# Value products of a head pair: one group in beat 4 instead of three groups in beats 0, 2 and 4

## What is computed

```python
def ffn(x):                       # W_fc 512x128, W_proj 128x512
    y = square(relu(x @ W_fc.T)) @ W_proj.T
    mem, spikes = 0, 0
    for _ in range(5):            # spiking neurons
        mem = 0.9 * mem + y - (mem > 1)
        spikes += (mem > 1)
    return spikes / 5
def attn(x):                      # 16 heads of 64, slopes 2**(-(h+1)/2)
    q, k, v = split(x @ w_qkv); q *= 64 ** -0.5
    sim = q @ k.T - abs(i - j) * slope[h]      # causal
    return (softmax(sim) @ v) @ w_out + b_out
x = x + 0.5 * ffn(layernorm(x))
x = x + attn(layernorm(x))
x = x + 0.5 * ffn(layernorm(x))
```

## Time and profile before

| | us |
|---|---|
| median of 3 runs | 1767.83 (1766.23 to 1768.95) |
| span of the profiled execution | 1764.1 |
| PE busy | 1676.8 (95%) |
| DVE busy | 1206.1 (68%) |
| ACT busy | 1289.0 (73%) |
| POOL busy | 920.2 (52%) |

### The profile page before, as it was taken

One profiled execution on the slowest core, in us unless ns is written; L12 is line 12 of the kernel. 1 busy time (PEld: TensorE's weight loads), 2 busy tenths in 40 slices (PEclk: granted clock), 3 DMA queues, 4 the chain that ended last, 5 costly groups with the idle time before them and its releaser, 6 DMA issues.

```text
span 1764.1 us, 39796 instructions
## 1 busy us (share of the span) xinstructions
PE 1676.8 (95%) x10902; PEld 1259.1 (71%) x10902; DVE 1206.1 (68%) x4272; ACT 1289.0 (73%) x3446; POOL 920.2 (52%) x1258
## 2 busy tenths in 40 slices
PE   4899999999999999999999999999999999999996
PEld 3767777677776777767777676776777677677775
DVE  6575776748777585775858768586785848767563
ACT  2687876777877787876877768687777868868781
POOL 2455554555545455545555545465454545546451
PEclk8999999999999999999999999999999999999998
DMA  2555453435434435443545434444443544434430
GB/s 73 114 109 111 85 119 75 102 82 109 101 81 107 89 84 108 92 104 76 105 93 107 96 82 107 90 87 107 90 103 78 109 95 94 102 82 101 94 82 13
DMA packets 80562, 164.80 MB, mean 93 GB/s; under 512 B 12880, under 2 KB 30928, under 8 KB 80208
## 3 DMA queue, kind: packets, MB, share of 16 engines
q1 hardware_dynamic: 80336, 162.12, 42.9%
HBM read 6.88 MB, written 4.19 MB: 6 GB/s over the span
## 4 chain that ended last, share of the span: by engine, by line
PE 69%; DVE 19%; issue 8%; POOL 2%; ACT 1%; DVEq 1%; DMA 1%; SPq 0%; POOLq 0%; ACTq 0%
PE bank L388 12%; PE bank L373 12%; PE bank L343 7%; PE bank L359 7%; PE bank L431 7%; PE bank L360 6%; PE bank L439 6%; PE bank L345 5%; PE bank L344 5%; DVE spikes L615 3%; DVE negsc L558 3%; DVE negmem L621 2%; DVE drive L618 2%; DVE xn L591 1%; DVE rsum L567 1%
## 5 line engine op out<-in xcount | busy, mean ns | idle before, releaser
L911 POOL TENSOR_TENSOR prob<-prob,rsum 128x512 f32<-128x512 f32 (+3 forms) x1024 | 731.7, 730 | 699.9 <-DVE rsum L567 699.6
L799 ACT ACTIVATE prob<-negsc,negmax 128x512 f32<-128x512 f32 (+3 forms) x1024 | 574.4, 565 | 124.2 <-DVE negmax L558 117.7
L810 ACT COPY probT<-bank 128x512 f32<-128x512 f32 x640 | 362.0, 587 | 194.5 <-PE bank L373 191.9
L558 DVE CUSTOM_DVE_ANT_0 negsc<-bank,alibi 128x512 f32<-128x512 f32 (+3 forms) x1024 | 466.2, 473 | 5.3 <-PE bank L360 5.3
L567 DVE RECIPROCAL rsum<-sums 128x1 f32<-128x1 f32 (+1 forms) x768 | 121.4, 158 | 483.3 <-PE bank L360 466.3
L373 PE MATMUL bank<-ident,prob 128*128 128x128 f32 x2560 | 373.6, 277 | 1.9 <-ACT probT L810 0.2
L359 PE MATMUL bank<-keys,queries 128*128 128x256 f32 (+2 forms) x1024 | 352.1, 355 | 23.1 <-DVE negmax L558 14.4
L388 PE MATMUL bank<-probT,vals 128*64 128x256 f32 (+3 forms) x2048 | 361.0, 453 | 0.3 <-ACT attT L817 0.3
L373 PEld LDWEIGHTS bank<-ident,prob 128*128 128x128 f32 x2560 | 296.2, 141 | 39.4 <-issue 28.6
L360 PE MATMUL bank<-keys,queries 128*128 128x256 f32 (+2 forms) x1024 | 321.2, 325 | 0.0
L359 PEld LDWEIGHTS bank<-keys,queries 128*128 128x128 f32 x1024 | 194.8, 190 | 74.6 <-DVE negmax L558 30.5
(11 more groups left out here) (82 smaller groups left out, 2246.3 us busy)
## 6 DMA issues: line engine op xcount, KB each, us to landing
queries<-queries SPq DMA_DIRECT2D x384, 256.0 KB, 3.0
keys<-k_lo SPq DMA_DIRECT2D x256, 128.0 KB, 2.4
keys<-keys SPq DMA_DIRECT2D x128, 128.0 KB, 3.7
x_in<-in_L_attn_x_dram SPq DMA_DIRECT2D x16, 256.0 KB, 2.9
out_dram<-x SPq DMA_DIRECT2D x16, 256.0 KB, 2.4
prob<-in_L_attn_w_qkv_dram SPq DMA_DIRECT2D x1, 1536.0 KB, 9.1
wo<-in_L_attn_w_out_dram SPq DMA_DIRECT2D x1, 512.0 KB, 10.7
probT<-in_L_ffn_W_fc_dram SPq DMA_DIRECT2D x1, 256.0 KB, 3.2
```

The source lines that it names most:

```text
L558: ins = dve.tensor_tensor_reduce(negsc[:, k % 3, col:col + WIDTH[i]], src, alibi[:, 2 * p + h, N - WIDTH[i]:N], 1.0, MASKED, ALU.add, ALU.min,
L799: ins = act.activation(prob[:, p % 2, h, PCOL[i]:PCOL[i] + WIDTH[i]], negsc[:, k % 3, col:col + WIDTH[i]], ACT.Exp, bias=negmax[:, p % 2, ...
L810: act.copy(probT[:, turn_slot(p, t), :], turn_bank[(len(TRUNS) * p + t) % 2][:, :]).then_inc(s_turned_out, 1)
L911: ins = pool.tensor_tensor(pr, pr, rsum[:, p % 2, seg:seg + 1].to_broadcast([P, WIDTH[i]]), ALU.mult)
```

## The change

The four value products of a pair, which stood in beat 0 (j=2), beat 2 (j=1 and 3) and beat 4 (j=0), now stand together in beat 4, in the order 0, 1, 2, 3. ACT's copy of the finished pair moves from beat 4 to beat 5. There it stands behind the probT copies of tiles 3 and 4 and ahead of the exponentials of beat 5. `PVORDER` and `PVLAST` follow from `PV`: the first product of the order, which clears the bank, is now j=0, and PE waits ahead of it for the last turned tile. `SIDE`, `TBEAT` and all else stay.

```diff
-ATTBEAT = 4
-PV = [[2], [], [1, 3], [], [0], []]
+ATTBEAT = 5
+PV = [[], [], [], [], [0, 1, 2, 3], []]
```

## The result

| | before | after |
|---|---|---|
| median | 1767.03 us (1765.58 to 1768.95) | 1802.93 us (1799.1 to 1808.93) |
| ratio, 95% interval | | 1.0207 [1.0187, 1.0227] |
| span of the profiled execution | 1764.1 us | 1797.0 us |
| forecast | | 1788.4 us, range 1754 to 1806 |

The change makes the kernel 2.1% slower. The sign and the mechanism of the forecast held; its rise of 20.6 us was too small. The rise was 36 us between the medians and 32.9 between the profiled spans. From there on, batch 0 is 0.4 us longer, the 14 batches behind it 33.9, and the tail 1.9: together 36.2.

The account below looks back on a forecast made before the run. PE has most of the chain, but DVE's unbroken stretches and side-bank margins cap its gains. A batch grows 1.4 us, times 14 is 19.6, plus 1 for the tail: span 1784.7, median 1788.4 us, range 1754 to 1806.

Parts of the forecast that it names:

- PE's saving: Value products: one group a slot costs 2.50 us instead of 3.16; 0.66 saved a slot, 84 over 128, none reaching the end.
- The copy's 0.47 in beat 5: ACT's moved pair copy delays exponentials and bank-freeing copies behind it by 0.47 us; its removal from beat 4 credits nothing.
- the ledger: PE's lead over the old timeline through a batch, by slot.beat (plus is earlier), capped by banks; ends at -1.4 us.
- Rival (b): ACT's moved copy costs nothing, using room left in beat 4: -0.2 to +0.3 us a batch, 1764 to 1771; chance 14%.
- 0.4: lead 0: Slot 0, beat 4: PE's lead starts at 0, since DVE's chain released PE there.
- 2.1 to 6.0: Slots 2 to 6: bank-capped leads of -0.22 at 2.1, +0.16 at 2.2, -1.12 at 3.0, -1.65 at 4.4, -0.91 at 6.0.
- 6.2: Slot 6, beat 2: at most 1.17 us gain, taken as 0.6 without a row; lead about -0.3, between -0.9 and 0.3.
- 6.3 to 0.4: DVE's chain into the next batch: loses 0.92 us at 6.5 and 0.2 at 7.1; lead -1.4 at next 0.4.
- The tail: Last pair's products all wait for its last probT copy: 0 to 1.3 us, taken as 1.
- Rival (c): Transposes of beats 1 and 2 also wait for POOL's normalising: 1.5 us a batch, 21 in all, 1809; chance 7%.
- Rival (a): PE bounds, drains are pure gain: 84 us less, 1684, chance 4%; half that gain or less, 1725 to 1763, 22%.
- The TensorE rule: Trainium skill: changing the array's tiling mode drains TensorE; two drains fewer a slot, 0.35 us per group beside its columns.

Follow-up runs that it names:

- the late copy: Changed kernel with ACT's copy of the finished pair moved from beat 5 to beat 2 of the next slot (pair 7 and tail unmoved): 1784.36 us, ratio 1.0102.
- the fastest kernel: Kernel before with only beat 0's product (j=2) moved to beat 4, ahead of j=0; pair copy stays in beat 4: 1752.35 us, ratio 0.9917.
- the kernel with 1775.78 us: Kernel with only j=2 moved from beat 0 to beat 4 (1752.35 us), its pair copy moved from beat 4 to beat 5: ratio 1.0059.

## Why the prediction was right, and where its terms were off

**PE's saving and that it doesn't arrive.** Right. The group costs what it was priced at, 2.31 us by the formula without neighbours and 2.31 by starts in the trace. The steps of the leads give the prices of beats 0, 2 and 4 to 0.01. L388's busy time fell by 57 us, the span rose.

**The copy's 0.47 in beat 5.** Right, and it is the largest term. In the ledger it is charged at 1.2, 2.1, 3.0 and in part at 7.1. Rival (b), the ledger without it, ends at -0.2 to +0.3, so the forecast gave the copy 1.2 to 1.7 us a batch, 17 to 24 us. Two single edits measured it: 18.6 us from the changed kernel, 23.4 from another. No run shows a gain from its absence in beat 4, which was assumed to be nothing.

**The rest of the loss.** This is the term that was mis-sized: the measured rise is 1.75 times the one forecast, and the time lies 3 us inside the upper end of the range. By (b)'s ledger the concentration of the products in beat 4 costs nothing; measured with the late copy it is 18 us. The table of leads puts the missing 1.0 us a batch at these steps:
- "0.4: lead 0" held. DVE's normalised x releases PE there in 8 of ten batches before and 7 of ten after, as shown above. What the forecast did not see is that the pause differs from batch to batch: from the scores of 0.4 to t1 it is 3.07 us in its batch (886.21 to 889.28), and 1.58 to 3.08 in ten batches, because the scores come later in some batches where the loop turns or the DMA of 0.0 is late.
- 2.1 to 6.0: at most 0.3 more than forecast, 0.14 of it left at 6.0. The caps are where I put them (fc at 1.2, out, y1, q and k, each waiting 0.5 to 0.6 or starting 0.05 after its bank), so the places were right.
- 6.2: this is the larger part, 0.7. I had no row for the cap and took 0.6 of gain, more than the 0.38 to 0.47 of the three places named beside it. Measured is -0.1. There are three tight banks in a row, k at 6.1 (relu copy), and both y3 tiles behind the low halves of q and k, and beat 2's gain of 1.17 is lost whole. The last of these margins stood in the trace of the kernel before:

```profile
964.64 3.74 PE L431 MATMUL bank<-wproj,hid 128*128 128x128 f32 x32
965.10 0.68 DVE L679 TENSOR_TENSOR k_lo<-bank,keys 128x512 fp32r<-128x512 f32 x1
```

  The second y3 tile, the last 16 of these 32 products, starts at 966.43, 0.65 after the end of k's low half, and k's own tile in 6.1 started 0.79 after its bank came free. The bound I gave for the lead after 6.2, -0.9, is what no gain at all from 6.0 on means. That end was the right one; it was even passed, with -1.16.
- 6.3 to 0.4: the stretch lost 1.24 where 1.1 was forecast. DVE's loss at 6.5 was worked out as 0.92 from the cover of 0.37. It is 0.89 in the row above, and 0.88 on average over ten batches. That leaves 0.36 for the low half of q at 7.1, taken as 0.2: DVE waits 0.46 there for ACT in every batch, where it didn't before.
- The tail was taken as 1 us and is 1.9. Of the 3.7 us between the span before and the median, 2.1 lie around the span and the rest is a difference between runs; this doesn't touch the rise.

**Rival (c), POOL at the turns,** was present in small: 11.3 us of waits at L373, 7.0 of it at 4.1, 0.5 in every batch. The wait for k's low half at 4.2 (0.76) follows right behind it, so the 0.5 is probably not lost on its own; this wasn't tested. The forecast's argument against it, that PE is late too, held for the rest. In the kernel with all products in beat 2 it became a main term.

**Rival (a)** failed as written. Its drains were real and PE's gain was real. But the fastest kernel shows what it is worth when the order lets it through: 14 us of 45 for one drain less, in the beat (0) whose emptying brings no wait at 2.2 and 4.2; nothing for the other (beat 2), which brings both.

**The TensorE rule.** The changed kernel agrees in kind with the page that speaks of a drain at a change of tiling mode (the Trainium skill, TensorEngine Tiling (Array Packing), Key Properties). By that rule fewer changes can only help, and that is true of PE's busy time in every kernel here (1626.6 to 1658.0 us, before 1676.8) and of the kernel's time in two (1752.35 and 1758.29 us).

**What stays open.** The two costs don't add up from single edits: beat 0 emptied gives -14 us, beat 2 emptied -1, both with the late copy +18. The tight banks behind a wholly emptied stretch are my explanation of the sign: both of them emptied bring waits at 2.1, 2.2, 4.2, 5.2 and 6.2 together. But the late copy in beat 2 may cost something itself, and no run separates the two. The longer DMA ahead of 0.0 has no cause here either.

## What to carry to other kernels

In a software pipeline with fixed queues, list for each tile the margin between its bank coming free and its start before an edit, and for every copy that moves count each of these margins that stands behind it: a delay of 0.47 us cost about 0.5 at every bank with a margin below that, three times a batch, 23 us in all. Bundling work saves its entry cost, but it empties the places it leaves; try the groups one by one, since the first gave 0.8% and the second nothing. Where a ledger has no row for a place, look for the row: the one guess without it held 0.7 of the missing 1.0 us. And count leads from an event that releases the engine, not from one that has slack behind it: counted from the scores of 0.4, the leads in the table above would all but the last be 0.45 lower, and would blame the wrong step.

## What the runs showed of the hardware

**The clock follows pauses of PE.** The cores' rows for the kernel before, for the late copy and for all products in beat 2, in that order:

```profile
core 0: 1764.1 us, clock 0.984
```

```profile
core 0: 1782.8 us, clock 0.979
```

```profile
core 0: 1823.0 us, clock 0.966
```

At 1.2 GHz for a share of twice what is missing to 1, these are 56, 75 and 124 us at the lower level. The 68 us more of the last kernel cost it at most 34 us (half of them, if PE was on the path all the time) of its 57 over the kernel before. Its own runs point to less: two at 0.966 took 1825 us and those at 0.972 and 0.973 took 1821 on average, which carried on to 0.984 is some 10 us (an estimate from these four runs). The pause of 2.10 us with the group of 4.06 behind it was shown above. An edit that makes PE idle in one place can so be charged again in the next; I had counted the idle time alone. The same pause of 2.1 us at 4.1 was followed by the lower level in nine of 14 batches and not in the other five. In the changed kernel no lower stretch in the middle batches stands behind the waits of 0.6 us; all stand at 0.0, where PE waits 1.9 to 4.4. Over the span its clock is 0.982, about 65 us at the lower level, some 8 more than before.

**A record isn't a cost.** ACT's copy of a bank shows 0.6 us in its record, and its neighbours start 0.47 to 0.48 later (802.18 to 802.66 in the kernel with 1775.78 us), the amount by which everything behind it moved.
